# Who issues the transfers of the maxima: SyncE's queue or GpSimd's

## The reference

```
x = x + _L0_attn_ref(_layernorm(x, axis=-1), ...)            # 256 keys
x = x + _L0_xattn_ref(_layernorm(x, axis=-1), ctx_1024, ...)  # 512 keys, a mask by key
...
x = x + _L3_attn_ref(_layernorm(x, axis=-1), ...)             # 256 keys, full mask
x = x + _L3_xattn_ref(_layernorm(x, axis=-1), ctx_1024, ...)  # 512 keys, full mask

    attn = softmax(q k^T * scale, with the mask)     # per head, width 8
    out  = (attn @ v, heads side by side) @ Wo
```

## Time and profile before

| | us |
|---|---|
| median of three runs | 1650.88 |
| the profiled execution, its own time | 1655.8 |
| its span, first to last instruction | 1653.6 |
| TensorE matmul busy | 1246.6 (75%) |
| VectorE busy | 940.7 (57%) |
| ScalarE busy | 689.8 (42%) |
| GpSimd busy | 250.6 (15%) |
| the four attentions with a maximum, from first to last second product of the group loop, roughly | 41 to 100, 149 to 252, 1328 to 1405, 1455 to 1574 |

### The profile page before, as it was taken

One profiled execution on the slowest core, in us unless ns is written; L12 is line 12 of the kernel. 1 busy time (PEld: TensorE's weight loads), 2 busy tenths in 40 slices (PEclk: granted clock), 3 DMA queues, 4 the chain that ended last, 5 costly groups with the idle time before them and its releaser, 6 DMA issues. The chain is left out here.

```text
span 1653.6 us, 25927 instructions
## 1 busy us (share of the span) xinstructions
PE 1246.6 (75%) x9204; PEld 762.3 (46%) x9248; DVE 940.7 (57%) x2485; ACT 689.8 (42%) x1299; POOL 250.6 (15%) x525
## 2 busy tenths in 40 slices
PE   3875997783975586556999999999667499679932
PEld 1332334681432386344666666666466233323311
DVE  5756773334744444655666766767420555667656
ACT  1643782221711121102666666666334145245612
POOL 1210111451000253100000000000055011111100
PEclk8896998897985699766999999999878689789965
DMA  5526110784230475000000000000165320431000
GB/s 130 141 68 144 31 65 25 223 267 119 35 108 0 135 256 173 3 1 0 1 1 1 1 1 1 2 1 1 33 190 177 103 60 3 97 82 17 2 13 13
DMA packets 77960, 112.58 MB, mean 68 GB/s; under 512 B 9881, under 2 KB 59270, under 8 KB 76982
## 3 DMA queue, kind: packets, MB, share of 16 engines
q1 hardware_dynamic: 73386, 101.81, 21.6%
q0 software_dynamic: 4448, 9.12, 1.8%
HBM read 85.79 MB, written 24.64 MB: 67 GB/s over the span
## 5 line engine op out<-in xcount | busy, mean ns | idle before, releaser
L540 DVE TENSOR_REDUCE mx<-ps 128x4 f32<-128x1024 f32 (+1 forms) x128 | 153.3, 1221 | 76.3 <-PE ps L482 68.3
L2047 DVE CUSTOM_DVE_ANT_0 wring<-ps,probs 128x768 f32<-128x768 f32 x128 | 122.6, 958 | 56.9 <-PE ps L1919 56.8
L679 PE MATMUL ps<-probs,vaug 128*32 128x256 f32 (+1 forms) x1792 | 143.3, 394 | 12.7 <-ACT probs L647 8.1
L2003 ACT COPY qs<-ps 128x768 f32<-128x768 f32 x128 | 102.3, 800 | 97.7 <-PE ps L1926 97.7
L637 ACT ACTIVATE probs<-ps 128x1024 f32<-128x1024 f32 x96 | 98.2, 1023 | 88.7 <-PE ps L515 88.7
L642 ACT ACTIVATE probs<-ps 128x512 f32<-128x512 f32 x192 | 106.2, 594 | 49.2 <-PE ps L599 46.8
L1985 ACT ACTIVATE wring<-wring,r 128x768 f32<-128x768 f32 x128 | 120.8, 944 | 2.9 <-DVE r L2050 2.9
L235 POOL TENSOR_TENSOR rstd<-veps,mhalf 128x8 f32<-128x8 f32 x14 | 23.2, 1657 | 619.5 <-DVE veps L220 592.2
L1926 PE MATMUL ps<-ident,wring 128*128 128x128 f32 x768 | 110.5, 281 | 3.2 <-DVE wring L2084 3.2
L482 PE MATMUL ps<-ks,qs 49*128 49x256 bf16 (+1 forms) x512 | 84.1, 370 | 28.0 <-DVE mx L535 11.9
L1926 PEld LDWEIGHTS ps<-ident,wring 128*128 128x128 f32 x768 | 84.6, 141 | 39.4 <-issue 35.3
(11 more groups left out here) (313 smaller groups left out, 2326.8 us busy)
## 6 DMA issues: line engine op xcount, KB each, us to landing
wring<-in_L_ffn_w SPq DMA_DIRECT2D x19, 768.0 KB
wring<-in_L_ffn_w SPq DMA_DIRECT2D x32, 384.0 KB
wring<-in_L_ffn_w SPq DMA_DIRECT2D x19, 514.0 KB
qs<-scr_q SPq DMA_DIRECT2D x30, 192.0 KB
scr_k<-probs SPq DMA_DIRECT2D x42, 128.0 KB, 3.2
scr_q<-probs SPq DMA_DIRECT2D x10, 384.0 KB, 3.1
probs<-in_L_ffn_w SPq DMA_DIRECT2D x8, 384.0 KB
probs<-in_L_ffn_w SPq DMA_DIRECT2D x4, 768.0 KB
```

What stands on the lines that cost most here:

```text
L540: dve.tensor_reduce(out, src, AX.X, ALU.max, negate=True).then_inc(a_max.sem, 1)
L679: ins = pe.matmul(ps[32 * j:32 * j + 32, self.av_bank(s), q0:S], vaug[:, s % 2, kt, j, :], probs[:, s % 2, j, at:at + S - q0], start=(kt = ...
L2003: act.copy(self.pT[:, g % 2, j, :, k * P:(k + 1) * P], self.buffer("turn", i, 0, KV).rearrange("p (t n) -> p t n", n=P)).then_inc(self.out ...
L2047: dve.tensor_tensor_reduce(self.sc[:, s, :], src, self.maskb[:, u // (2 * PR), :], 1.0, -3.0e38, ALU.add, ALU.max, self.top[:, s:s + 1]).t ...
```

## The change

The two transfers of each group are no longer issued by SyncE but by GpSimd, on its own DMA queue, and stand in GpSimd's program where the list says "turn", behind a wait for `m_sb`. SyncE keeps its wait for `m_sb` of each group, and all its other transfers in the same order. Nothing else is edited; line numbers behind the first hunk shift (L553 is L549 in the changed kernel, L581 is L585, L444 is L578).

```diff
@@ -438,10 +438,6 @@
             for g in range(G):
                 sp.wait_ge(m_sb.sem, m_sb.at(self.n, g + 1))
-                at = (g // NQ * PAIRS + g % NQ * 2) * S
-                for r in range(2):
-                    row = HALF * r + ROWS_A
-                    sp.dma_start(qs[row:row + 3, at:at + 2 * S], mT[6 * r:6 * r + 6, g % 2, :]).then_inc(m_in[g % 4].sem, 16)
                 if self.n == 0:
                     late_inputs(sp, g)
@@ -572,6 +568,14 @@
+        def maxima_gpsimd(self, pool, s):
+            n = self.n
+            pool.wait_ge(m_sb.sem, m_sb.at(n, s + 1))
+            at = (s // NQ * PAIRS + s % NQ * 2) * S
+            for r in range(2):
+                row = HALF * r + ROWS_A
+                pool.dma_start(qs[row:row + 3, at:at + 2 * S], mT[6 * r:6 * r + 6, s % 2, :]).then_inc(m_in[s % 4].sem, 16)
@@ -899,6 +903,8 @@
                     self.values_gpsimd(pool, (s - self.behind) // self.u)
+                if what == "turn":
+                    self.maxima_gpsimd(pool, s)
                 if what == "split":
                     self.split_gpsimd(pool, s)
```

## The result

| us | before | changed |
|---|---|---|
| median of four runs each, side by side | 1652.41 (1649.08 to 1657.03) | 1685.28 (1679.49 to 1686.20) |
| ratio, with its 95% interval | | 1.0174 [1.0144, 1.0205] |
| span of the profiled execution | 1653.6 | 1684.3 |
| granted clock, mean of the span | 0.852 | 0.843 |
| L0_attn | 104.3 | 121.6 |

The ratio is that of the record, with its interval; it is not the quotient of the two medians, which is 1.0199.

What follows compares the result with a forecast made beforehand. It took TensorE's waits for m_in, 23.1 us in all, as what the transfers could affect; 9 + 6 + 7 + 1 = +23 us on the median of 1650.88 gave 1674 us, range 1642 to 1698.

Steps and rivals of the forecast that it cites:

- The 23 us: Forecast total loss over the four attentions: 9 in L0_attn, 6 in L0_xattn, 7 in L3_xattn, 1 in L3_attn.
- What bounds the kernel: Moved transfers matter only through m_in, for which TensorE waits at second products; 23.1 us, 1.4%, could be gained at most.
- The price of an issue, 0.96 us: Each plain DMA on GpSimd costs 0.96 us, taken from its indirect DMAs; bounds 0.50 and 1.23.
- The 0.30 between the two: Gap of 0.30 us between the pair's two issues on GpSimd, part of the 2.49 us pair.
- the crossing at 1.83: Pair time of 1.83 us, 0.63 per issue, where the 23 us loss over about 35 pairs crosses zero.
- rival 1: Plain DMA is cheap on GpSimd, 0.50 us an issue: kernel faster by 12 us, 1639 us; chance 0.16.
- The L0_attn loop, +9: In L0_attn, turn, copy, pair and split form a GpSimd loop of 4.48 us against 3.26: +9 us.
- A landing stall in each group of L0_xattn and L3_xattn, +12 and +10: Late m_in stalls TensorE 1.24 us in L0_xattn, 1.0 in L3_xattn, ten times each: +12.4 and +10.
- Gains at the heads of attentions: In L0_xattn the first product starts 3.9 us earlier, as SyncE's issue no longer waits behind spills.
- The loads that stood behind them start about 1.4 us earlier: SyncE's loads behind the removed issues start about 1.4 us earlier; costed at nothing.
- Rival 4: Own queue brings no relief, as transfer engines full of loads delay landings: +9 us on top, 1683 us; chance 0.13.
- The clock: A lower granted clock as TensorE idles more: not counted, only widens the upper side of the range.

Runs made afterwards that it cites:

- e3: Kernel before, with GpSimd also issuing an unread twin of each pair while SyncE still issues the real ones first: 1639.04 us, 1.0033.
- e4: Kernel before, with GpSimd issuing only group 0's two transfers in each attention, SyncE the other fifteen groups': 1635.76 us, 0.9995.
- e7: Changed kernel, with SyncE waiting for the pair's landing before anything large and loads of batches 2 and 3 spread over four groups each: 1653.34 us, 1.0014.
- e6: Kernel before, with the eight loads of batches 2 and 3 cut over four groups each, each part behind a group's pair: 1641.31 us, 0.9940.
- e5: Changed kernel unedited, measured once more against the kernel before: 1684.51 us against 1651.81, 1.0186.
- e1: Changed kernel, with SyncE waiting for m_in (the group's pair landed) where it waited for m_sb: 1658.23 us against 1637.09, 1.0132.
- e8: Kernel before, with ScalarE issuing each pair on its own hardware queue right after writing mT, nothing on GpSimd: 1720.32 us, 1.0422.

## Why the prediction was right in its sign and wrong in its reason

That 1685 lies between 1642 and 1698 is luck. The 23 us were added up from an issue and a landing that are both dearer than they are here, and with the measured ones the same sum gives no loss. What costs the time stands in the text at nothing.

**What bounds the kernel.** Held as to the place: the sublayers between the attentions are within some 4 us of before. The loss went through `m_in`, for which TensorE waits, as the text says, but also through TensorE's clock.

**The price of an issue, 0.96 us.** Wrong: 0.57. The 0.30 between the two isn't there either, and the first starts 0.64 us after the copy, not 0.27. The indirect DMAs were the wrong neighbour; SyncE's 0.695 for the very same shape was the nearer one, and the lower bound of 0.50 the nearest. The text said that an issue under 0.63 makes the forecast wrong, and it is. By the sum as written, a pair of 1.76 lies under the crossing at 1.83: 35 x (1.76 - 1.83) = -2, a kernel slightly faster. It became 33 us slower. (The range, too, was read wrongly: it doesn't take in rival 1, whose 1639 lies below 1642.)

**The L0_attn loop, +9.** The loop exists (GpSimd's L552 now ends TensorE's wait in some steps) at 3.52 us instead of 4.48, worth at most 0.26 x 15 = 4. Besides the pair, the way from the turn to `mT` was too long in the sum, 0.96 where the step above has 63.07 - 62.39 = 0.68: 0.68 + 1.76 + 1.04 = 3.48. The sublayer lost 17.3.

**A landing stall in each group of L0_xattn and L3_xattn, +12 and +10.** About 0.22 us in a plain step of the first and nothing in the second, and most of the 0.22 is there in e3 too, whose real pairs land by the old path. A landing takes 1.7 us from an issue's start, where 0.96 + 1.42 = 2.38 was assumed; 1.1 of them are behind the issue's end, not 1.42.

**Gains at the heads of attentions.** The first wait of L0_xattn fell from 5.72 to 3.75, and in e4 to 3.85: 2 us where 3.9 were counted. The issue was cured of its lateness, the landing only half. And the second wait grew from 1.67 to 3.31, so the first two steps take 20.3 us against 19.6: there was no gain. The wait behind the loads of a batch did not go at all, 4.68 us where 3.70 stood.

**"The loads that stood behind them start about 1.4 us earlier. I cost that at nothing, since no second product of those batches is near."** This is the step that failed. I looked for a product that *needs* those loads, and there is none near; what mattered is what the loads run *beside*: the group's own small pair. A transfer that starts 1.4 us earlier passed the pair that used to be ahead of it. The changed kernel with order kept and loads spread (e7) is at 1.0014, the one with the loads spread alone (e10) at 1.0309. How many of the change's own 33 us are the order's is an estimate: some 20, if the 12 that e7 has above e6 are taken off, though the wait of e7 and the move need not add up so. It shows in L0_attn at the late inputs, in L0_xattn at the spill (12.20 us between copies where 6.92 stood), in L3_attn (7.91 where 4.67 stood, 6.18 in e5) and L3_xattn at the loads.

**The rivals.** Rival 4 (0.13, 1683 us) is nearest in time and in kind: the transfer engines were full of loads, not SyncE's line too long. It still missed that the old line was protecting the pair. The rule of the Trainium skill that it rests on ("DMA: Bandwidth & Descriptors", section "Issuing engines are not separate DMA queues"), that DMAs issued by different engines run on the same 16 DMA engines and interleave, agrees with the rows at 191 to 199 us, where a pair issued from another engine than the loads took 5.75 us to land.

**The clock.** It was "not counted" and only widened the upper side. In L0_attn it goes with the larger part, 13.4 us of matmul time against 4.8 us of added waits.

## What to carry to other kernels

Where one engine issued a small urgent transfer and then large ones behind the same semaphore, its program order acted as a priority (e6 against e10). Moving the small one to a queue of its own gives that priority away, even if its own issue gets cheaper, since both queues are released at once and the large one may be first. Before splitting a queue, list what is released by the same event and ask which leaves first; then either keep the order or hold the large one back, and cut it into pieces that end before the next urgent one. Holding back alone was not enough here (e1, 1.0132), cutting alone gave 0.6% (e6). And price a wait of TensorE in a busy stretch above its length: two of them cost 1.7 times theirs here.

## What the runs showed that I had not expected

A plain DMA of this shape costs GpSimd 0.57 us to issue, against 0.70 on SyncE and 0.73 on ScalarE, while its indirect ones take 0.98; the first starts 0.64 us after ScalarE's copy ends.

The landing of a transfer of the pair came 1.6 to 6.9 us after its issue on GpSimd's queue, which carried nothing else in these stretches. On ScalarE's queue, TensorE's waits for the pair were 15.9 us in all against 38.7 on GpSimd's (28.9 and 9.8). Whether that queue is served better beside large transfers, or ScalarE's slower pace in e8 only left more room, no run here tells apart.

One wait of 3.61 us left TensorE at the lower clock level through the next two windows of 8 us, though it was busy in both of them from end to end.
